# Routing and expert tiles of a mixture layer in one phase, with the first weights, the slot table and the output copy rearranged

## The reference

```
# x: 1024 x 512; router_w 8 x 512; w_gate, w_up 8 x 1024 x 512; w_down 8 x 512 x 1024
xn = layernorm(x)
routing = softmax(xn @ router_w.T)              # 1024 x 8
top_w, top_i = top_k(routing, 2);  top_w /= sum(top_w)
combine[n, top_i] += top_w                      # 1024 x 8
h = silu(xn @ w_gate[e].T) * (xn @ w_up[e].T)   # per expert e
out = x + sum_e combine[:, e] * (h @ w_down[e].T)
```

## Time and profile before

| what | us |
|---|---|
| median of 3 runs | 1825.94 (1825.88 to 1828.14) |
| profiled execution | 1827.44 |
| its span, first to last instruction | 1825.6 |
| mixture, from its first instruction to the end | 1330.3 to 1825.6 |
| expert tiles, PE's first product to its last | 1391.9 to 1810.6 |

### The profile page before, as it was taken

How to read it: one execution, slowest core, us unless ns; L and a number is a source line. 1 busy time by engine, 2 the same in 40 slices (tenths; PEclk the granted TensorE clock), 3 DMA queues, 4 the chain that set the end, 5 groups by cost and what they waited for, 6 DMA issues and landing times. The chain is left out here.

```text
span 1825.6 us, 26717 instructions
## 1 busy us (share of the span) xinstructions
PE 1686.1 (92%) x9168; PEld 1447.6 (79%) x9168; DVE 1098.1 (60%) x2221; ACT 858.7 (47%) x1195; POOL 451.3 (25%) x332
## 2 busy tenths in 40 slices
PE   5999999999998599989997998999955999999996
PEld 4899999999997488778886886788844888888885
DVE  5445555555554666653336666433355999999993
ACT  3444444344443432353334223533314888787883
POOL 0334443444333343300003342000001122121211
PEclk9999999999999799899999998999956999999998
DMA  4111001110100500022224000223134334646612
GB/s 160 47 36 36 26 32 35 35 35 24 33 23 0 187 1 0 1 81 99 98 73 148 1 0 1 93 93 102 35 110 161 103 101 153 202 134 222 230 45 64
DMA packets 35200, 139.65 MB, mean 76 GB/s; under 512 B 4672, under 2 KB 5312, under 8 KB 28416
## 3 DMA queue, kind: packets, MB, share of 16 engines
q1 hardware_dynamic: 29984, 126.75, 19.2%
q0 software_dynamic: 5152, 12.06, 3.4%
HBM read 222.42 MB, written 12.85 MB: 129 GB/s over the span
## 5 line engine op out<-in xcount | busy, mean ns | idle before, releaser
L1687 DVE TENSOR_TENSOR e_w<-e_raw,e_w 128x2048 fp32r<-128x2048 f32 x138 | 311.5, 2287 | 21.9 <-ACT e_w L1631 21.9
L1631 ACT ACTIVATE e_w<-e_raw 128x2048 fp32r<-128x2048 f32 x138 | 264.2, 1917 | 58.6 <-DMA e_raw<-in_we 32.8
L78 PE MATMUL bank<-e_w,e_xT 128*128 128x512 f32 x1104 | 274.0, 398 | 1.4 <-DVE e_xT L1705 1.4
L78 PEld LDWEIGHTS bank<-e_w,e_xT 128*128 128x128 f32 x1104 | 206.6, 191 | 43.1 <-DVE e_xT L1705 1.8
L78 PE MATMUL bank<-ctx,wk 128*128 128x258 f32 x1536 | 194.1, 286 | 3.9 <-PEq L179 3.9
L78 PE MATMUL bank<-x2T,fw 128*128 128x512 f32 x768 | 188.9, 396 | 6.1 <-DVE fw L1094 6.1
L1252 PE MATMUL bank<-fw,hh 128*128 128x512 f32 x768 | 186.8, 393 | 5.3 <-DVE hh L1123 5.3
L78 PEld LDWEIGHTS bank<-ctx,wk 128*128 128x128 f32 x1536 | 188.3, 191 | 4.0 <-issue 4.0
L78 PE MATMUL bank<-wv,ctx 128*128 128x512 f32 x768 | 189.3, 395 | 0.0
L78 PEld LDWEIGHTS bank<-x2T,fw 128*128 128x128 f32 x768 | 147.0, 192 | 37.7 <-DVE fw L1094 6.6
L1252 PEld LDWEIGHTS bank<-fw,hh 128*128 128x128 f32 x768 | 144.5, 189 | 36.9 <-DVE hh L1123 6.9
(11 more groups left out here) (221 smaller groups left out, 2736.2 us busy)
## 6 DMA issues: line engine op xcount, KB each, us to landing
e_raw<-in_we SPq DMA_DIRECT2D x138, 1024.0 KB
fraw<-in_wf SPq DMA_DIRECT2D x64, 512.0 KB, 3.3
ctxraw<-in_ctx SPq DMA_DIRECT2D x32, 514.0 KB, 3.3
wraw<-in_wa SPq DMA_DIRECT2D x20, 512.0 KB, 5.1
X<-in_x SPq DMA_DIRECT2D x2, 1024.0 KB, 6.5
xh_d<-A SPq DMA_DIRECT2D x8, 256.0 KB, 2.4
acc_d<-X SPq DMA_DIRECT2D x8, 256.0 KB, 3.0
out<-acc_d SPq DMA_DIRECT2D x4, 512.0 KB, 5.6
```

Of the source, the lines that this page charges most:

```text
L78: last = nc.tensor.matmul(out, lhs(t, a), rhs(t, b), start=start and n == 0, stop=n == len(steps) - 1)
L1631: nc.scalar.activation(w[pos][:, 0, :, :], raw[pos][:, :, :], ACT.Copy).then_inc(m["w_hi"], 1)
L1687: nc.vector.tensor_tensor(w[pos][:, 1, :, :], raw[pos][:, :, :], r(w[pos][:, 0, :, :]), ALU.subtract).then_inc(m["w_lo"], 1)
```

## The change

The two blocks of `mixture` become one, so their barrier goes, and six things move with it:

1. SP loads the five weight pieces G0, U0, G1, U1, D0 of expert 0 at the start of the block, ahead of the stores. When tile 0's expert is known, the same pieces are requested again under the condition "the expert is not 0". The sixth piece (D1) has its first load after the routing, since its buffer holds routing data.
2. `group_expert` (the chain `ge`, `gsum`, `gmin`) stands behind the slot table's operands.
3. `carried` and `row_hot` are written in fp32r (the rounded format in which one pass is enough). The share is split into a rounded part and a remainder, so `carried` has three parts of 24 columns (`NGE`), 72 columns instead of 46.
4. POOL computes the two share parts of `carried`; DVE writes `row_hot` in two halves, and the products of the first half wait for that half alone.
5. The last tile's result isn't added to `acc_d`. SP copies `acc_d` to `out` after the 22nd addition; POOL gathers the last tile's rows of `acc_d` into `A[:, 7]`; DVE adds the tile's result to them; POOL scatters the sum to `out`, and rows above 1023 (the spare slots) are left out by a bounds check.
6. `row_hot` lies in the buffer of D1's rounded weights, the router's turned tiles (`xr`) and the zeros (`none`) in D1's raw buffer.

```diff
@@ routing constants and buffers @@
+NGE = NG + NG % 2
-            row_hot = sbi("row_hot", [P, 2 * NT, P])
-            group_hot = sbi("group_hot", [P, 2 * NT, NG])
-            carried = sbi("carried", [P, 2 * NT, 2, NG])
+            group_hot = sbi("group_hot", [P, 2 * NT, NGE])
+            carried = sbi("carried", [P, 2 * NT, 3, NGE], F32R)
+            share_hi = sbi("share_hi", [P, 2 * NT], F32R)
+            share_lo = sbi("share_lo", [P, 2 * NT])
+            row_hot = w[D1][:, 0, :, :].rearrange("p c n -> p (c n)").rearrange("p (k n) -> p k n", n=P)
+            xr = [raw[D1][:, i, :] for i in range(3)]
+            none = raw[D1][:, 3, :]
@@ sync @@
+                    sp.dma_start(tab[:, :], a["route_tab"]).then_inc(q["tab_in"], 16)
+                    sp.dma_start(rw[:, :, :], a["rw"]).then_inc(q["tab_in"], 16)
+                    for pos in (G0, U0, G1, U1, D0):
+                        sp.dma_start(raw[pos][:, :, :], a["we"][0, PIECE_AT[pos], :, :].rearrange("p (c n) -> p c n", c=DC)).then_inc(w_in[pos], 16)
...
-                        if owner > 0:
+                        if owner == 0 and pos == D1:
+                            sp.wait_ge(q["logit_ps"], NT)
+                            sp.wait_ge(q["none_stored"], 32)
+                        elif owner == 0:
+                            sp.wait_ge(w_in[pos], 16)
+                        else:
                             sp.wait_ge(m["w_lo"], done(g - 1, pos))
...
-                    expert, changed = expert_of(0), None
+                    sp.wait_ge(q["expert_ok"], 1)
                     for g in range(NG):
-                        if g >= 1:
-                            before, expert = expert_of(g - 1), expert_of(g)
-                            changed = expert != before
+                        before, expert = expert_of(g - 1) if g else 0, expert_of(g)
+                        changed = expert != before
...
-                    sp.wait_ge(m["y_added"], 16 * NG)
+                    sp.wait_ge(m["y_added"], 16 * (NG - 1))
                     rows = TOK // 4
                     for i in range(4):
                         sp.dma_start(out[i * rows:(i + 1) * rows, :], acc_d[i * rows:(i + 1) * rows, :]).then_inc(m["copied"], 16)
-                    sp.wait_ge(m["copied"], 16 * 4)
+                    sp.wait_ge(m["placed"], 16)
@@ gpsimd @@
+                    pool.wait_ge(q["share_ok"], 1)
+                    pool.wait_ge(q["group_ok"], 1)
+                    for v, part in ((1, r(share_hi[:, :])), (2, share_lo[:, :])):
+                        nc.gpsimd.tensor_tensor(carried[:, :, v, :], group_hot[:, :, :], part.unsqueeze(2).broadcast_to([P, 2 * NT, NGE]),
+                                                ALU.mult).then_inc(q["carried_ok"], 1)
...
+                    pool.wait_ge(stored[0], 16 * NT)
+                    pool.wait_ge(q["none_stored"], 32)
+                    pool.wait_ge(q["token_ok"], 1)
                     gather(0)
                     gather(1)
+                    pool.wait_ge(stored[1], 16 * NT)
...
-                    scatter(NG - 1)
-                    pool.wait_ge(m["y_added"], 16 * NG)
+                    pool.wait_ge(m["y_added"], 16 * (NG - 1))
+                    nc.gpsimd.indirect_dma_start(out=last_acc, out_offset=None, in_=acc_d[:, :],
+                                                 in_offset=bass.IndirectOffsetOnAxis(ap=token[:, NG - 1:NG], axis=0)).then_inc(m["acc_in"], 16)
+                    pool.wait_ge(m["y_ok"], NG)
+                    pool.wait_ge(m["copied"], 16 * 4)
+                    nc.gpsimd.indirect_dma_start(out=out[:, :], out_offset=bass.IndirectOffsetOnAxis(ap=token[:, NG - 1:NG], axis=0),
+                                                 in_=yb, in_offset=None, bounds_check=TOK - 1, oob_is_err=False).then_inc(m["placed"], 16)
+                    pool.wait_ge(m["placed"], 16)
@@ scalar @@
-                    result(NG - 1, PIECES * NG)
@@ vector @@
+                    link(nc.vector.tensor_copy(share_hi[:, :], shares))
+                    nc.vector.tensor_tensor(share_lo[:, :], shares, r(share_hi[:, :]), ALU.subtract).then_inc(q["share_ok"], 1)
...
+                    dve.wait_ge(m["step_ps"], PIECES * NG)
+                    dve.wait_ge(m["acc_in"], 16)
+                    nc.vector.tensor_tensor(yb, bank[4][:, :], last_acc, ALU.add).then_inc(m["y_ok"], 1)
@@ tensor @@
-                    pe.wait_ge(m["rows_ok"], 1)
-                    pe.wait_ge(m["carried_ok"], 2)
-                    for n in range(2 * NT):
-                        last = nc.tensor.matmul(bank[5][:, 0:2 * NG], row_hot[:, n, :], carried[:, n, :, :].rearrange("p v g -> p (v g)"),
-                                                start=n == 0, stop=n == 2 * NT - 1)
+                    pe.wait_ge(q["carried_ok"], 3)
+                    for k in range(2):
+                        pe.wait_ge(q["rows_ok"], k + 1)
+                        for n in range(k * NT, (k + 1) * NT):
+                            last = nc.tensor.matmul(bank[5][:, 0:3 * NGE], row_hot[:, n, :], carried[:, n, :, :].rearrange("p v g -> p (v g)"),
+                                                    start=n == 0, stop=n == 2 * NT - 1)
```

More of the change, by code:

```diff
@@ new lines, in normalise @@
+                    def normalise(i):
+                        dve.wait_ge(q["rs_ok"], i + 1)
+                        for t in parts[i]:
+                            nc.vector.tensor_scalar(A[:, t, :], X[:, t, :], mv[:, t, 0:1], rstd[:, t:t + 1], ALU.subtract, ALU.mult).then_inc(q["xh_ok"], 1)
+                    add(0)
+                    statistics(0)
+                    add(1)
+                    normalise(0)
+                    statistics(1)
+                    normalise(1)
+                    dve.wait_ge(q["logit_ps"], NT)
@@ new lines, in _ @@
+                    link(nc.vector.tensor_copy(rank[:, :, :], counted(0)))
+                    step[0] += 1
+                    dve.wait_ge(q["route"], step[0])
+                    for i, back in enumerate((1, 2, 4)):
+                        link(nc.vector.tensor_tensor(cum[1 - i % 2][:, 4:, :], cum[i % 2][:, 4:, :], cum[i % 2][:, 4 - back:4 + NT - back, :], ALU.add))
+                    total = cum[1][:, 3 + NT, :]
+                    link(nc.vector.tensor_tensor(full[:, :, :], total.unsqueeze(2).broadcast_to([P, NE, TOK // GT]),
+                                                 steps.unsqueeze(1).broadcast_to([P, NE, TOK // GT]), ALU.is_gt))
@@ new lines, in _ @@
+                    link(nc.vector.scalar_tensor_tensor(where[:, 1, :, :], gs[:, 0, :].unsqueeze(1).broadcast_to([P, NT, NE]), float(GT),
+                                                        where[:, 0, :, :], ALU.mult, ALU.add))
+                    for k in range(2):
+                        link(nc.vector.tensor_tensor(picked[:, k, :, :], hot[:, k, :, :], where[:, 1, :, :], ALU.mult))
+                    link(nc.vector.tensor_reduce(slotf[:, :, :], picked[:, :, :, :], AX.X, ALU.add))
+                    link(nc.vector.tensor_copy(slot[:, 0, :], slotf[:, :, :].rearrange("p k t -> p (k t)")))
@@ new lines, in _ @@
+                    nc.vector.tensor_tensor(offset[:, :], ids.rearrange("p k t -> p (k t)"), place[:, 0, :], ALU.subtract).then_inc(q["route"], 1)
+                    dve.wait_ge(q["group_ok"], 1)
+                    dve.wait_ge(q["route"], step[0])
+                    nc.vector.tensor_tensor(carried[:, :, 0, :], group_hot[:, :, :], offset[:, :].unsqueeze(2).broadcast_to([P, 2 * NT, NGE]),
+                                            ALU.mult).then_inc(q["carried_ok"], 1)
+                    for k in range(2):
+                        nc.vector.tensor_tensor(row_hot[:, k * NT:(k + 1) * NT, :], place[:, 0, k * NT:(k + 1) * NT].unsqueeze(2).broadcast_to([P, NT, P]),
+                                                iota_p.unsqueeze(1).broadcast_to([P, NT, P]), ALU.is_equal).then_inc(q["rows_ok"], 1)
@@ L1685, in split_lo @@
+                    dve.wait_ge(q["table_ps"], 1)
+                    nc.vector.tensor_scalar(token[:, :], bank[5][:, 0:NG], spare, None, ALU.add).then_inc(q["token_ok"], 1)
+                    link(nc.vector.tensor_copy(gate[:, :], bank[5][:, 2 * NGE:2 * NGE + NG]))
+                    link(nc.vector.tensor_tensor(gate[:, :], bank[5][:, NGE:NGE + NG], gate[:, :], ALU.add))
                     def split_lo(g, pos):
```

286 lines of the change are left out of this document (117 added, 169 removed).

## The result

| | before | after |
|---|---|---|
| median, us | 1826.52 (1825.88 to 1828.14, 4 runs) | 1814.60 (1812.21 to 1817.22, 4 runs) |
| ratio after to before | | 0.9934, 95% interval 0.9916 to 0.9952 |
| profiled execution, us | 1827.44 | 1817.22 |
| its span | 1825.6 | 1815.3 |

The median fell by 11.9 us, to 1814.60. The forecast was 1812.6, a gain of 13.3, with a range of 1806 to 1819. In a later set of runs the same two kernels gave 1827.87 (11 runs) and 1812.98 (6 runs), ratio 0.9926 (0.9914 to 0.9938).

A forecast was written before the change was run, and what follows sets the result against it. PE bounds the expert tiles, so only the front before its first product and the tail behind its last can move. Front 8.0 plus tail 5.3 is 13.3 us: 1825.94 - 13.3 = 1812.6, range 1806 to 1819.

The forecast's parts named there:

- The tiles stay: Expert tiles: PE is busy 20.00 of 20.00 us at full clock, so their time doesn't change (gain 0).
- `place` earlier by 1.17: Front, DVE: the four expert instructions move behind `row_hot`, so `place` ends 1.17 us earlier; two new share instructions cost nothing.
- Operands and products: Front: DVE and POOL take turns on operands until 1372.3; 16 fp32r products at 0.22 each end at 1375.8, against 1380.2.
- Barrier, 1.2: Front, between `token` and the first gather: POOL waits for `token_ok` alone, 0.3 us instead of 1.48, gaining 1.2.
- Gather, 5.0: Front, first gather: 5.0 us from issue to landing instead of 7.39, with five loads already done, gaining 2.4.
- Weights hidden: Front: DVE's split of G0 ends at 1382, before the turned tile is split, hidden with 1.1 us to spare.
- Tail, 5.3: After PE's last product: copies, scatter, then POOL's DRAIN end at 1820.3 against 1825.6, a gain of 5.3 us.
- the step that I held for easy to miss: End of the block: POOL's DRAIN of 3.8 us, before hidden under SP's wait for the copies, is no longer hidden.
- Mild port and DRAIN: Rival: POOL slips between DVE's instructions (1.5 us) and the final DRAIN is short (3.8), giving 1807.3; chance 0.18.
- Slow narrow products: Rival: narrow fp32r table products are slow and D1's load holds the gather, losing 3.8 and 2.4, giving 1818.8; chance 0.12.
- No overlap: Rival: in the tail, copies and last gather share transfer engines, so only the front gains, giving 1817.9; chance 0.08.
- Clock: Rival: PE's clock rises later in tiles 0 and 1, each product of 12 costing 2.75 us more, giving 1831.9; chance 0.03.

The follow-up runs named there:

- shares on DVE: The two share products of `carried` moved from POOL to DVE, against the changed kernel: front 54.10 us against 54.41.

## Why the prediction was right, and where it was off

Runs of their own show the worth of the rounded table, of the loads beside the gather, of POOL's share and of the end. The order of `group_expert` and the missing barrier have no run of their own; their worth is read from the two profiles.

- *The tiles stay.* 418.67 against 418.89: right.
- *`place` earlier by 1.17.* Measured 1.25, the two share instructions hidden (DVE's wait ahead of the counts shrank from 0.75 to 0.27): right.
- *Operands and products.* I had the products end 4.4 us earlier, with the two engines taking turns; measured 4.93. The collision is real (shares on DVE), but I had it too long: from `group_hot`'s end to the first product it is 3.3 us, not 3.9. POOL's first product took 0.83, not 1.04, and beside POOL's two DVE lost 1.28 (0.65 in `carried`, 0.63 in `row_hot`, all of that in its first half), not 2.08. (By my own terms a front without collision would have been 1.7 shorter, not the 1.5 that I wrote.) A record of 0.22 for a rounded product was right: 3.60 / 16 = 0.225. The Trainium skill (SBUF — State Buffer, Who interferes with whom) states that a DVE instruction with two SBUF inputs contends with a GpSimd instruction that reads SBUF. The trace agrees: the same instruction took 1.21 beside POOL and 0.56 without it.
- *Barrier, 1.2.* This term was mis-sized. From `token`'s end to the gather's issue it is 0.92, not 0.3, so only 0.56 was gained. I had taken POOL's usual 0.3 ahead of an indirect transfer; 0.84 of it is listed as issue. The trace of before had the same stretch, in its chain of waits, between POOL's release from the barrier and the first gather:

```profile
1381.06 0.02 POOLq L1360
1381.08 0.88 issue
1381.96 7.39 DMA A<-xh_d,token
```

  So of the 1.48 only 0.60 stood ahead of that release and could go. The wait alone doesn't make this stretch: the addition at 1811.49, which had waited for ACT, started 0.27 after its release. What POOL does in it is open.
- *Gather, 5.0.* Mis-sized too: 5.73, since D1's load was issued at 1378.95, almost together with it, and not 1.1 behind it. Without that load 3.6.
- *Weights hidden.* Right: DVE had split G0 at 1381.55, 2.9 us before the gather had even landed.
- *Tail, 5.3.* Measured 5.62. Copies 9.85 us instead of 9.3, POOL 0.9 from their landing to the scatter, the scatter landed 2.1 after its issue instead of 3.9, and the DRAIN 3.9. The errors nearly cancel, so the closeness of 5.3 is in part luck. The 2.1 belongs to a scatter that places nothing, since the last tile holds no token with these inputs; with tokens in it the scatter moves rows, and no run shows what that takes. That the DRAIN comes out from under the copies, the step that I held for easy to miss, was right: without scatter and DRAIN the tail is 1.99.
- *The rivals.* Mild port and DRAIN: out, both effects are there, the port's at 0.6 less than I had it. Slow narrow products: out (0.225), but the other half, D1 holding the gather, was partly true. No overlap: out. Clock: the first product took 5.50 at half clock against 5.49, and no more of them; the clock showed in the routing instead, by 1.2 us from one execution to another.

The sum: 8.0 was 7.15, by the barrier (-0.6) and the gather (-0.7) against the products (+0.5); 5.3 was 5.6.

## What to carry to other kernels

Loading weights ahead paid here through what it took away from a gather on the critical path, not through the weights; so hold back whatever else would run beside such a small transfer, even one load. Moving work to another engine has to be read in both engines' durations: the helper's time came back as longer instructions on the helped one. And when a new last instruction is made, look for what used to hide under the old one, an engine's drain above all.

## What the runs showed of the hardware

- POOL's DRAIN after indirect transfers: it ended 3.8 to 3.9 us after POOL was free, or 1.9 us after the landing where that was later (the second in two kernels); without them it took 0.04 at the ends of two phases and ended 0.1 after POOL's work in the routing block.
- The first gather of 128 rows of 2 KB landed in 3.5 to 3.6 us without a load beside it, 5.7 to 5.8 beside one 1 MB load issued at the same time, and 7.4 to 7.7 beside six. The last gather, beside 2 MB of copies, took 6.9 to 7.5 with one issuing queue and 10.0 with two (one run).
- A product and two one-hot writes on DVE grew from 2.9 us (0.56 + 2.35) to 4.2 (1.21 + 2.98) beside POOL's two.
- In unchanged routing code the granted clock was 0.50 in nine executions, and near 1.00 for some 3 us in four, whose stage was 1.1 to 1.2 us shorter.
